# A GRU scan and a mixture of experts on one core: one scale for x, other chunk ends, and a step with its elementwise work dealt out anew

## The chip, the core and the metric

The kernel runs on one NeuronCore of a Trainium2 chip. The core has TensorE (PE, matrix products), VectorE (DVE), ScalarE (ACT, activation functions), GpSimd (POOL) and SyncE (SP), which here only issues DMA transfers. Each engine works through its own instructions in order; engines wait for each other by counting semaphores. The metric is the time of one launch in device microseconds.

## What is computed

The reference runs a GRU cell over x (4 x 512 x 512), started from `cond`, sends the states through a layer of four experts and adds the result to x:

```python
def cell(h, x):
    gi = x @ W_ih + b_ih
    gh = h @ W_hh + b_hh
    i_r, i_z, i_n = jnp.split(gi, 3, axis=-1)
    h_r, h_z, h_n = jnp.split(gh, 3, axis=-1)
    r = jax.nn.sigmoid(i_r + h_r)
    z = jax.nn.sigmoid(i_z + h_z)
    n = jnp.tanh(i_n + r * h_n)
    h_new = (1.0 - z) * n + z * h
    return (h_new, h_new)
...
for i in range(E):                       # E = 4 experts, the top 2 for each token, 512 tokens each
    sel_p, sel_idx = jax.lax.top_k(score, capacity)
    tok = flat_x[sel_idx]
    h = jax.nn.gelu(tok @ W1[i], approximate=False)
    y = h @ W2[i] * p
    out = out.at[sel_idx].add(y)
return x + out
```

## The kernel before

**Steps.** The 512 time steps of each of the 4 sequences are cut into 16 segments of 32 steps, and all 64 segments run at once as 64 columns. A segment starts from a guessed state, so 40 steps run before the 32 whose states are kept (`FIRST` = 40, `L` = 32, 72 in all), and a check at the end asks whether the segments' ends meet their neighbours' starts; only if not would further rounds of 32 steps run. The 512 hidden units are four blocks of 128 rows, j = 0 to 3. The states are held times a power of two, s.

**Numbers in halves.** Matrix products run in fp16. A number is kept as a high half and a low half (what the high one leaves). The first 20 steps (`ROUGH`) multiply high halves alone. From step 20 a step has 144 recurrent matmuls (128 x 64 columns, line 400): for each pair (j, k) six with the high half of state block k (`HIGH`, both halves of the weights, three gates) and three with its low half (`LOW`). The input gates r and z of the step, computed in advance, are added by a product with a diagonal matrix (`inject`, line 410: a matmul for the high and one for the low part, called a pair of injections here). `ORDER` writes out in what order TensorE takes these units.

**A step on the other engines.** When gate block j is complete, ScalarE makes the sigmoids r and z (`sig`, line 673), VectorE the product with r (`reset`, 1078) and the candidate's input (`candidate_in`, 1083), ScalarE the tanh (678), VectorE (z-1) times the candidate (`one_less_z`, 1087), GpSimd z times the old state (`carry`, 815). VectorE's `blend` (1094) gives the high half of the new state block, -s (z-1) n + z h, and releases the next step's `HIGH` units for this k; `keep_state` (1099) gives the same sum in fp32. The low halves are made by GpSimd for blocks 0 and 1 (823) and by VectorE for 2 and 3 (1118), as `LOW_BY = "PPDD"` says. Each engine has the order of these operations written out; TensorE waits for `high_ready`, `low_ready` and, before an injection, for `rn_done`.

**Input gates.** x @ W_ih for the step's inputs is computed in four chunks of 8 steps. The first chunk is done in fp32 at the start (lines 365 and 375); the rest, called the fill (line 392, 128 x 512), is spread over steps 0 to 22: 24 matmuls ahead of step 0, then 18 with each step, 13 of them at its head. ScalarE stores each finished tile (627, 630), VectorE makes its high half (`rz_high`, 986, a copy) and its low part (`rz_low`, 993); TensorE needs the high halves of a chunk when the chunk begins (steps 8, 16, 24), and from step 24 all low parts too. W_hh's low halves (`whh_low`, 1061) are made in twelve pieces between steps, as `WHH_AT` says. In all of these VectorE does the extra work after the step's own (`other_work`).

**Preparation.** Before anything is scaled, VectorE finds the largest magnitudes (944, 949, 959, 1010, 1029), GpSimd takes the maximum over partitions, and VectorE turns it into a power of two. x has two scales, `X0` for its first two chunks and `X1` for the others, so that the second is found later (1029).

**After the steps** come the transposition of the states, the choice of the tokens, and four experts with the products of lines 564 and 577. None of that is touched.

## Time and profile before

| | |
|---|---|
| three runs | 900.26, 902.24, 902.24 us (median 902.24) |
| the profiled execution | 901.38 us, span 899.6 us |
| PE busy | 808.9 us (90%) |
| DVE busy | 634.0 us (70%) |
| ACT busy | 414.9 us (46%) |
| POOL busy | 181.9 us (20%) |

The span is the time from the first to the last instruction, and the rest of an execution's time lies around it. The stages are: preparation up to 62.8 us, steps 0 to 19 and the filled steps 20 to 22 up to about 202, the plain steps up to about 459, then the choice of the tokens, and from 548 the experts. Matmuls are pipelined, so that a busy PE isn't one at its peak: the time between the starts of instructions tells more than their durations.

### The profile page before, as it was taken

How to read it: one execution, taken by the hardware profiler on the slowest of the kernel's cores; microseconds unless marked ns; L12 is line 12 of the kernel's file. 1: busy time of each engine (PE TensorE's matmuls, PEld its weight loads, DVE VectorE, ACT ScalarE, POOL GpSimd, SP SyncE). 2: the span in 40 equal slices, each digit the busy share in tenths (PEclk: the TensorE clock that was granted, in tenths of full speed). 3: DMA queues.
4: the chain of work that ended last, by engine and by line, in shares of the span. 5: the costliest groups of instructions: out<-in, count | busy, mean ns of one | idle time of the engine just before them, and what ended most of it. 6: DMA issues, size and time to landing. Idle time of an engine off the chain costs nothing.

```text
span 899.6 us, 28130 instructions
## 1 busy us (share of the span) xinstructions
PE 808.9 (90%) x11698; PEld 531.5 (59%) x11699; DVE 634.0 (70%) x2083; ACT 414.9 (46%) x852; POOL 181.9 (20%) x458
## 2 busy tenths in 40 slices
PE   7979899997999999999954147999999999999996
PEld 3436565687999899999944134444444444444442
DVE  5968898876888888888855865767666765774500
ACT  0767575653545545455423304834373257406600
POOL 1012121222433334333310010022002101120011
PEclk9999999998999999999978557999999999999999
DMA  8800000000000000000031740437152706350011
GB/s 322 333 0 3 2 2 1 2 3 3 4 5 4 4 4 4 5 4 4 4 131 60 226 174 24 141 95 211 24 182 63 210 12 202 84 169 13 1 24 23
DMA packets 20646, 62.58 MB, mean 70 GB/s; under 512 B 2160, under 2 KB 2160, under 8 KB 18032
## 3 DMA queue, kind: packets, MB, share of 16 engines
q1 hardware_dynamic: 16224, 52.47, 17.0%
q0 software_dynamic: 3584, 8.42, 5.2%
q8 instruction: 85, 1.39, 0.7%
q14 instruction: 33, 0.27, 0.1%
q10 hardware_dynamic: 720, 0.03, 0.1%
HBM read 52.49 MB, written 12.62 MB: 72 GB/s over the span
## 4 chain that ended last, share of the span: by engine, by line
PE 70%; DVE 20%; issue 5%; ACT 2%; DMA 1%; POOL 1%; DVEq 0%; SPq 0%; POOLq 0%
PE ps L564 19%; PE ps L577 18%; PE ps L400 18%; PE ps L392 8%; DVE wa L1078 4%; DVE wa L1083 3%; DVE halves L1094 3%; ACT wa L673 2%; PE ps L410 2%; PE ps L506 2%; DVE ocand L1087 1%; PE ps L552 1%; PE ps L544 1%; DMA big<-in_w_ih 1%; DVE chunk_peak L1010 1%
## 5 line engine op out<-in xcount | busy, mean ns | idle before, releaser
L400 PE MATMUL ps<-halves,wa 128*128 128x64 f16 x8448 | 289.8, 194 | 7.6 <-DVE halves L1094 1.4
L400 PEld LDWEIGHTS ps<-halves,wa 128*128 128x128 f16 x8448 | 273.4, 98 | 34.9 <-DVE halves L1094 15.9
L564 PE MATMUL ps<-wb,big 128*128 128x512 f16 x768 | 168.8, 382 | 1.5 <-DVE wb L1382 1.5
L577 PE MATMUL ps<-big 128*128 128x512 f16 x768 | 166.9, 379 | 0.0
L673 ACT ACTIVATE wa<-ps,un_gates 128x128 f32<-128x128 f32 x288 | 100.2, 366 | 126.5 <-PE ps L400 120.1
L564 PEld LDWEIGHTS ps<-wb,big 128*128 128x128 f16 x768 | 75.2, 98 | 93.1 <-issue 4.4
L577 PEld LDWEIGHTS ps<-big 128*128 128x128 f16 x768 | 75.2, 98 | 89.9
L678 ACT ACTIVATE wa<-wa,un_gates 128x64 f32<-128x64 f32 x288 | 99.1, 344 | 57.9 <-DVE wa L1083 51.4
L1078 DVE SCALAR_TENSOR_TENSOR wa<-ps,bhn_s,wa 128x64 f32<-128x64 f32 x288 | 80.0, 278 | 63.9 <-ACT wa L673 63.7
L392 PE MATMUL ps<-hx,wb 128*128 128x512 f16 x432 | 108.5, 384 | 4.9 <-issue 4.9
L740 ACT ACTIVATE hx<-ps,un_hid_in 128x512 f32<-128x512 f32 x64 | 43.7, 683 | 114.3 <-PE ps L564 112.0
L1094 DVE SCALAR_TENSOR_TENSOR halves<-ocand,neg_scale,wa 128x64 f16<-128x64 f32 (+1 forms) x288 | 86.5, 300 | 3.9
L1274 DVE SCALAR_TENSOR_TENSOR big<-wa,scale,big 128x2048 f16<-128x2048 f32 x28 | 65.3, 2350 | 26.0 <-ACT big L726 26.0
L726 ACT ACTIVATE big<-wa,scale 128x2048 f16<-128x2048 f32 x32 | 62.5, 1988 | 44.5 <-DVEq L1262 44.5
L1395 DVE SCALAR_TENSOR_TENSOR big<-hx,hid_scale,big 128x512 f16<-128x512 f32 x64 | 47.9, 749 | 44.3 <-ACT big L743 33.9
L1233 DVE TENSOR_REDUCE chunk_peak<-wa 128x1 f32<-128x2048 f32 x32 | 71.1, 2276 | 0.0
L410 PE MATMUL ps<-big,diag 128*128 128x128 f16 x496 | 62.4, 221 | 8.1 <-DVE big L986 8.0
L1083 DVE TENSOR_TENSOR wa<-wa,big 128x64 f32<-128x64 f32 x288 | 65.9, 229 | 5.1
L1087 DVE SCALAR_TENSOR_TENSOR ocand<-wa 128x64 f32<-128x64 f32 x288 | 62.6, 217 | 0.0
L392 PEld LDWEIGHTS ps<-hx,wb 128*128 128x128 f16 x432 | 38.4, 99 | 40.7 <-issue 7.9
L815 POOL TENSOR_TENSOR wa<-wa,hx 128x64 f32<-128x64 f32 x128 | 42.6, 333 | 78.6 <-ACT wa L673 74.0
L873 POOL DMA_INDIRECT out<-hx,idx_out x16 | 29.1, 1816 | 135.6 <-DVE hx L1401 135.6
(180 smaller groups left out, 685.7 us busy)
## 6 DMA issues: line engine op xcount, KB each, us to landing
wa<-in_w SPq DMA_DIRECT2D x32, 1024.0 KB, 7.3
hs_rows<-big SPq DMA_DIRECT2D x8, 516.0 KB, 6.4
hx<-in_x_t SPq DMA_DIRECT2D x3, 1024.0 KB, 18.6
big<-in_w_hh SPq DMA_DIRECT2D x4, 768.0 KB, 15.1
big<-in_w_ih SPq DMA_DIRECT2D x2, 1024.0 KB, 10.1
wa<-in_x_t SPq DMA_DIRECT2D x4, 256.0 KB, 4.8
big<-in_w_ih SPq DMA_DIRECT2D x4, 256.0 KB, 7.0
hx<-hs_rows,idx POOLq DMA_INDIRECT x16
```

Of the source, the lines that this page charges most:

```text
L392: mm = pe.matmul(ps[:, gi_bank(tile), :], wih_parts[:, w, k, m * P:(m + 1) * P], x_parts[:, q, t, k, :], start=(left == 0), stop=(left == ...
L400: mm = pe.matmul(gate_ps[:, j, g, :], whh_parts[:, k, w, (4 * g + j) * P:(4 * g + j + 1) * P], halves[:, src, k, h, :], start=False, stop= ...
L410: pe.matmul(gate_ps[:, j, 0:2, :], diag[:, 1 if c in (1, 2) else 0, :], gi_rz[:, c, j, part, :, cols], start=(part == HIGH), stop=False, s ...
L564: mm = pe.matmul(ps[:, m % 2, :], w1p[:, w, k, m * P:(m + 1) * P], tokT[:, t, k, :], start=(k == 0 and n == 0), stop=(k == KD - 1 and n == 2))
L577: mm = pe.matmul(ps[:, 2 + g % 2, :], hid[:, h, k, g * P:(g + 1) * P], w2p[:, w, k, :], start=(k == 0 and n == 0), stop=(k == KH - 1 and n ...
L673: act.activation(rz[:, j, :, :], gate_ps[:, j, 0:2, :], ACT.Sigmoid, scale=un_gates[:, 0:1]).then_inc(S["sig_done"], 1)
L678: act.activation(cand[:, j, :], cand_in[:, j, :], ACT.Tanh, scale=un_gates[:, 0:1]).then_inc(S["tanh_done"], 1)
L1078: dve.scalar_tensor_tensor(rn[:, j, :], gate_ps[:, j, 2, :], bhn_s[:, j:j + 1], rz[:, j, 0, :], ALU.add, ALU.mult).then_inc(S["rn_done"], 1)
L1083: dve.tensor_tensor(cand_in[:, j, :], rn[:, j, :], gi_n(j), ALU.add).then_inc(S["candin_ready"], 1)
L1087: dve.scalar_tensor_tensor(ocand[:, j, :], rz[:, j, 1, :], -1.0, cand[:, j, :], ALU.add, ALU.mult).then_inc(S["ocand_done"], 1)
L1094: dve.scalar_tensor_tensor(high_of(j), old(ocand_, j), neg_scale[:, 0:1], old(zh_, j), ALU.mult, ALU.add).then_inc(S["high_ready"], 1)
L1233: dve.tensor_reduce(chunk_peak[:, c:c + 1], stage[:, c * CHUNK:(c + 1) * CHUNK], AX.X, ALU.max, apply_absolute_value=True).then_inc(S["chu ...
```

## The change

Five things are done.

1. x has one scale (`XS`) for all chunks: all of x is loaded ahead of W_hh and its peak found ahead of the first scale; the late peak, the second gate scale and the second diagonal matrix go. The first x and W_ih loads go in halves instead of quarters, those of W_ih from ScalarE's queue.
2. ScalarE makes the high halves of five instead of eight tiles of the first chunk, VectorE the other three.
3. In the last step of a chunk the copy `rz_high` stands ahead of the step instead of behind it (`ahead`), and at the last filled step (23) `rz_low` too. W_hh's low pieces come one to a step, from step 0 on. The wait for all twelve pieces in ScalarE's step 16 becomes a wait in each of the tiles that overwrite them.
4. In the steps ScalarE makes s(1-z) = -s z + s (`kept_of`, tile `wz`, with scale and bias from columns), so that `one_less_z` is a plain product, and `blend` and `keep_state` plain sums. The product waits for `wz_done` as well.
5. GpSimd makes three of the four low halves, and `ORDER` and VectorE's order of a step are others.

```diff
-        ORDER = ((INJECT, 0, 0), (INJECT, 1, 0), (HIGH, 1, 0), (INJECT, 2, 0), (HIGH, 0, 0), (HIGH, 2, 0),
...
+        ORDER = ((INJECT, 2, 0), (INJECT, 0, 0), (INJECT, 1, 0), (HIGH, 1, 0), (HIGH, 0, 0), (HIGH, 2, 1), (INJECT, 3, 0),
...
-        WHH_AT = {5: (0, 1), 6: (2, 3), 7: (4, 5), 8: (6, 7), 13: (8, 9), 14: (10,), 15: (11,)}
+        WHH_AT = dict(zip((0, 1, 5, 6, 7, 8, 13, 14, 15, 16, 17, 18), range(WHH_PIECES)))
+        ACT_HIGHS = 5
-        LOW_BY = "PPDD"
+        LOW_BY = "PPPD"
...
+                def kept_of(j):
+                    act.wait_ge(S["sig_done"], base + j + 1)
+                    act.activation(wz[:, j, :], rz[:, j, 1, :], ACT.Identity, bias=scale[:, STATE:STATE + 1],
+                                   scale=neg_scale[:, 0:1]).then_inc(S["wz_done"], 1)
...
                 def one_less_z(j):
                     dve.wait_ge(S["tanh_done"], base + j + 1)
-                    dve.scalar_tensor_tensor(ocand[:, j, :], rz[:, j, 1, :], -1.0, cand[:, j, :],
-                                             ALU.add, ALU.mult).then_inc(S["ocand_done"], 1)
+                    dve.wait_ge(S["wz_done"], base + j + 1)
+                    dve.tensor_tensor(ocand[:, j, :], wz[:, j, :], cand[:, j, :], ALU.mult).then_inc(S["ocand_done"], 1)
                 def blend(j):
...
-                    dve.scalar_tensor_tensor(high_of(j), old(ocand_, j), neg_scale[:, 0:1], old(zh_, j),
-                                             ALU.mult, ALU.add).then_inc(S["high_ready"], 1)
+                    dve.tensor_tensor(high_of(j), old(ocand_, j), old(zh_, j), ALU.add).then_inc(S["high_ready"], 1)
...
-            for n in range(2, NC_):
-                dve.wait_ge(S["x_loaded"][n], 16)
-            link(dve.tensor_reduce(peak[:, X1:X1 + 1], hx[:, 2 * KD * GCOLS:KD * N], AX.X, ALU.max,
-                                   apply_absolute_value=True))
...
                 if i < FILLED:
                     for t in range(split_by(i - 1), split_by(i)):
                         if TILES[t][1] < 8:
-                            between += [(rz_high, t), (rz_low, t)]
+                            (ahead if s == STEPS_C - 1 else between).append((rz_high, t))
+                            (ahead if i == FILLED - 1 else between).append((rz_low, t))
```

ScalarE in a step, before: four sigmoids (L673 before, L670 after) and four tanhs (L678, L675).

```order
L673 ACTIVATE wa<-ps,un_gates 128x128 x3
L678 ACTIVATE wa<-wa,un_gates 128x64 x2
L673 ACTIVATE wa<-ps,un_gates 128x128
L678 ACTIVATE wa<-wa,un_gates 128x64 x2
```

And after:

```order
L670 ACTIVATE wa<-ps,un_gates 128x128 x2
L679 ACTIVATE wz<-wa,scale,neg_scale 128x64
L670 ACTIVATE wa<-ps,un_gates 128x128
L675 ACTIVATE wa<-wa,un_gates 128x64 x2
L679 ACTIVATE wz<-wa,scale,neg_scale 128x64
L670 ACTIVATE wa<-ps,un_gates 128x128
L675 ACTIVATE wa<-wa,un_gates 128x64
L679 ACTIVATE wz<-wa,scale,neg_scale 128x64 x2
L675 ACTIVATE wa<-wa,un_gates 128x64
```

The four new activations (L679) stand behind sigmoid 1, behind tanh 1, and two behind tanh 2.

TensorE in a plain step, before (L410 and L411 are injections, L400 and L401 recurrent matmuls):

```order
L410 MATMUL ps<-big,diag 128x128 x4
L400 MATMUL ps<-halves,wa 128x64 x6
L410 MATMUL ps<-big,diag 128x128 x2
L400 MATMUL ps<-halves,wa 128x64 x12
L410 MATMUL ps<-big,diag 128x128 x2
L400 MATMUL ps<-halves,wa 128x64 x126
```

And after:

```order
L411 MATMUL ps<-big,diag 128x128 x6
L401 MATMUL ps<-halves,wa 128x64 x18
L411 MATMUL ps<-big,diag 128x128 x2
L401 MATMUL ps<-halves,wa 128x64 x126
```

Three pairs of injections now stand ahead of the first unit. The last six of the 18 matmuls are `(HIGH, 2, 1)`, the first to need the second blend, so that it is wanted 12 matmuls behind the first one instead of 18. Behind its start 63 matmuls come until gate block 0 is complete, as before, but now with the last pair of injections among them. Behind gate block 0 there are 69 instead of 63; of these, blocks 1 and 2 are complete after 12 and 33 (before 15 and 27).

VectorE between steps 22 and 23, before: the low halves of step 22, copy and low part of one gate tile, and step 23's first reset; the last tile's copy and low part come behind step 23 in the same way.

```order
L1118 TENSOR_TENSOR halves<-carried,halves 128x64 x2
L986 CAST big<-gi_full 128x512
L993 TENSOR_TENSOR big<-gi_full,big 128x512
L1078 SCALAR_TENSOR_TENSOR wa<-ps,bhn_s,wa 128x64
L1083 TENSOR_TENSOR wa<-wa,big 128x64
```

And after, with both tiles ahead of step 23's first reset (L1068) and nothing behind its low half:

```order
L1106 TENSOR_TENSOR halves<-carried,halves 128x64
L987 CAST big<-gi_full 128x512
L994 TENSOR_TENSOR big<-gi_full,big 128x512
L987 CAST big<-gi_full 128x512
L994 TENSOR_TENSOR big<-gi_full,big 128x512
L1068 SCALAR_TENSOR_TENSOR wa<-ps,bhn_s,wa 128x64
L1073 TENSOR_TENSOR wa<-wa,big 128x64
```

## Rows read from the trace of the kernel before

**Rows 1.** windows by stage: length, busy us of each engine, granted clock, DMA share, GB/s

```profile
48.30:62.80 14.50, 9.64 (x38) 4.06 (x38) 9.06 (x21) 10.15 (x13) 2.78 (x5) 0.88 0.00 1
62.80:181.10 118.30, 114.67 (x1503) 71.00 (x1502) 100.17 (x387) 73.01 (x198) 24.69 (x82) 1.00 0.01 2
```

**Rows 2.** chain of waits, steps 20 and 49: start us, us, what

```profile
179.21 3.67 PE ps L400 x126
182.89 3.88 PE ps L392 x18
...
339.20 0.11 PE ps L410 x2
```

**Rows 3.** timeline, ScalarE in one plain step: start us, us

```profile
336.68 1.15 ACT L673 ACTIVATE wa<-ps,un_gates 128x128 f32<-128x128 f32 x3 [1.60 <-PE ps L400]
337.74 0.73 ACT L678 ACTIVATE wa<-wa,un_gates 128x64 f32<-128x64 f32 x2
...
341.78 1.16 ACT L673 ACTIVATE wa<-ps,un_gates 128x128 f32<-128x128 f32 x3 [1.60 <-PE ps L400]
```

**Rows 4.** timeline, VectorE and GpSimd in that step

```profile
337.13 1.13 POOL L815 TENSOR_TENSOR wa<-wa,hx 128x64 f32<-128x64 f32 x3 [1.60 <-ACT wa L673]
...
338.19 0.21 DVE L1087 SCALAR_TENSOR_TENSOR ocand<-wa 128x64 f32<-128x64 f32 x1
...
338.51 0.28 DVE L1094 SCALAR_TENSOR_TENSOR halves<-ocand,neg_scale,wa 128x64 f16<-128x64 f32 x1
...
339.24 0.41 DVE L1094 SCALAR_TENSOR_TENSOR halves<-ocand,neg_scale,wa 128x64 f16<-128x64 f32 x1
339.27 0.30 POOL L823 TENSOR_TENSOR halves<-hx,halves 128x64 f16<-128x64 f32 x1
```

**Rows 5.** groups by shape: xcount, busy us, mean ns, idle before

```profile
L678 ACT ACTIVATE wa<-wa,un_gates 128x64 f32<-128x64 f32 x192 | 65.8, 343 | 36.5 <-DVE wa L1083 34.4
...
L627 ACT ACTIVATE gi_full<-ps,bias_gi,gi_scale 128x512 f32<-128x512 f32 x8 | 6.1, 767 | 25.0 <-DVEq L980 22.0 <-DVE big L993 2.9
...
L627 ACT ACTIVATE gi_full<-ps,bias_gi 128x512 f32<-128x512 f32 x2 | 1.4, 688 | 2.1 <-PE ps L392 1.9 <-issue 0.3
```

**Rows 6.** timeline, step 0 and the chunk ends at steps 8 and 16

```profile
65.49 0.88 ACT L673 ACTIVATE wa<-ps,un_gates 128x128 f32<-128x128 f32 x3 [4.56 <-PE ps L400]
...
69.17 0.29 DVE L1094 SCALAR_TENSOR_TENSOR halves<-ocand,neg_scale,wa 128x64 f16<-128x64 f32 x1
...
109.39 0.23 PE L410 MATMUL ps<-big,diag 128*128 128x128 f16 x1 [2.31 <-DVE big L986]
...
150.60 0.89 ACT L673 ACTIVATE wa<-ps,un_gates 128x128 f32<-128x128 f32 x3 [0.70 <-PE ps L400]
...
157.61 0.88 ACT L673 ACTIVATE wa<-ps,un_gates 128x128 f32<-128x128 f32 x3 [3.13 <-PE ps L400]
```

**Rows 7.** timeline and a window, the chunk end at step 24

```profile
201.95 1.16 ACT L673 ACTIVATE wa<-ps,un_gates 128x128 f32<-128x128 f32 x3 [0.36 <-PE ps L400]
...
206.91 0.42 DVE L986 CAST big<-gi_full 128x512 f16<-128x512 f32 x1
...
208.16 0.58 PE L410 MATMUL ps<-big,diag 128*128 128x128 f16 x4 [4.42 <-DVE big L986]
...
208.00:214.00 6.00, 5.84 (x103) 5.87 (x103) 0.06 (x1) 0.37 (x1) 0.03 (x1) 0.50 0.01 3
...
218.92 0.37 ACT L673 ACTIVATE wa<-ps,un_gates 128x128 f32<-128x128 f32 x1 [1.60 <-PE ps L400]
```

**Rows 8.** chain of waits, then timeline, preparation

```profile
12.21 2.29 DVE chunk_peak L944
...
38.77 4.41 DVE L1029 TENSOR_REDUCE peak<-hx 128x1 f32<-128x4096 f32 x1
...
51.67 1.41 DVE L1004 SCALAR_TENSOR_TENSOR hx<-hx,scale 128x512 f16<-128x512 f32 x2
...
53.18 9.83 PE L392 MATMUL ps<-hx,wb 128*128 128x512 f16 x37 [4.86 <-issue]
```

More of the change, by code:

```diff
@@ L31 @@
 HIDDEN_TO = float(2.0 ** -16)
-WHH, STATE, W1, W2, WIH, X0, BIAS, X1 = range(8)
+WHH, STATE, W1, W2, WIH, XS, BIAS = range(7)
 SEARCH_BITS = 3
@@ L211, in gru_moe @@
         S["wih_loaded"] = [sem(f"wih_loaded_{g}") for g in range(3)]
-        S["first_loaded"] = [sem(f"first_loaded_{k}") for k in range(KD)]
+        S["first_loaded"] = [sem(f"first_loaded_{k}") for k in range(2)]
         S["whh_loaded"] = [sem(f"whh_loaded_{k}") for k in range(KD)]
-        S["x_loaded"] = [sem(f"x_loaded_{n}") for n in range(NC_)]
+        S["x_loaded"] = [sem(f"x_loaded_{n}") for n in range(1, NC_ + 1)]
         block = ctx.enter_context(nc.Block())
@@ L302, in _ @@
         def _(sp):
-            for k in range(KD):
-                sp.dma_start(x_first[:, k, :], x_t[:, CHUNK_ORDER[0], k, :]).then_inc(S["first_loaded"][k], 16)
-                sp.dma_start(wih_sb[:, k, 0:D], wih_src[:, k, 0:D]).then_inc(S["first_loaded"][k], 16)
+            for k in range(2):
+                sp.dma_start(x_first[:, 2 * k:2 * k + 2, :], x_t[:, CHUNK_ORDER[0], 2 * k:2 * k + 2, :]
+                             ).then_inc(S["first_loaded"][k], 16)
             for g in range(1, 3):
@@ L409, in inject @@
                 for part in parts:
-                    pe.matmul(gate_ps[:, j, 0:2, :], diag[:, 1 if c in (1, 2) else 0, :], gi_rz[:, c, j, part, :, cols],
+                    pe.matmul(gate_ps[:, j, 0:2, :], diag[:, :], gi_rz[:, c, j, part, :, cols],
                               start=(part == HIGH), stop=False, skip_group_check=True)
@@ L591, in _ @@
         def _(act):
+            for k in range(2):
+                act.dma_start(wih_sb[:, 2 * k:2 * k + 2, 0:D], wih_src[:, 2 * k:2 * k + 2, 0:D]
+                              ).then_inc(S["first_loaded"][k], 16)
             act.dma_start(bih[:, :], b_ih).then_inc(S["small_loaded"], 16)
@@ L617, in x_high, with keep_tile @@
                 act.activation(x_parts[:, q, HIGH, k, :], xT[:, q + 1, k, :], ACT.Copy,
-                               scale=x_scale(q)).then_inc(S["x_high"], 1)
-            def keep_tile(t, q, sc, g_sc):
+                               scale=scale[:, XS:XS + 1]).then_inc(S["x_high"], 1)
+            def keep_tile(t, sc, g_sc):
                 c, m = TILES[t]
@@ L651, in _ @@
                 first_tile(m)
+                first_high(m)
             for k in range(KD):
                 wih_high(k)
-            act.wait_ge(S["x_loaded"][1], 16)
             for k in range(KD):
                 x_high(0, k)
-            first_tile(3)
-            first_tile(4)
+            for m in range(3, ACT_HIGHS):
+                first_tile(m)
+                first_high(m)
             act.wait_ge(S["gates_known"], 1)
-            whh_high(0)
-            first_tile(5)
-            whh_high(1)
-            first_tile(6)
-            whh_high(2)
-            first_tile(7)
-            whh_high(3)
-            for m in range(8, 12):
+            for k in range(KD):
+                whh_high(k)
+            for m in range(ACT_HIGHS, 12):
                 first_tile(m)
@@ L1062, in whh_low, with step @@
                                          whh_parts[:, k, HIGH, cols], ALU.mult, ALU.subtract).then_inc(S["whh_ready"], 1)
-            def step(gi_n, after, src, base, low, moved=False, between=()):
+            def step(gi_n, after, src, base, low, moved=False, ahead=(), between=()):
                 dst = 1 - src
@@ L1127, in step @@
                          (one_less_z, 2), (blend, 2), (one_less_z, 3), (blend, 3), (other_work, 0))
+                for f, n in ahead:
+                    f(n)
                 for n, (f, j) in enumerate(exact if low else rough):
@@ L1165, in _ @@
                     after = lambda j, i=i: hs[:, j, i - FIRST + 1, :]
-                between = []
+                ahead, between = [], []
                 if i < FILLED:
@@ L1169, in _ @@
                         if TILES[t][1] < 8:
-                            between += [(rz_high, t), (rz_low, t)]
+                            (ahead if s == STEPS_C - 1 else between).append((rz_high, t))
+                            (ahead if i == FILLED - 1 else between).append((rz_low, t))
                 if 1 <= s <= KD and q < 2:
                     between.append((x_low, (q + 1, s - 1)))
-                for n in WHH_AT.get(i, ()):
-                    between.append((whh_low, n))
-                step(lambda j, c=c, cols=cols: gi[:, c, j, 2, cols], after, i % 2, KD * i, i >= ROUGH - 1, moved, between)
+                if i in WHH_AT:
+                    between.append((whh_low, WHH_AT[i]))
+                step(lambda j, c=c, cols=cols: gi[:, c, j, 2, cols], after, i % 2, KD * i, i >= ROUGH - 1, moved, ahead, between)
             def run(steps):
```

152 lines of the change are left out of this document (72 added, 80 removed).

## The prediction

> **What bounds the kernel now.** The table of windows comes first: through the filling steps (62.80 to 181.10) TensorE counts as busy for 114.7 of 118.3 us at full granted clock, while at the end of the preparation (48.30 to 62.80) it is busy for only 9.6 of 14.5 us, at 0.88 [rows 1]. A busy TensorE is not the answer by itself, so the second view is one plain step (24 to 71). A recurrent matmul costs 0.029 us (126 in 3.67), a filling matmul 0.216 (18 in 3.88), a pair of injections 0.11 [rows 2]. A plain step has 144 recurrent matmuls and 4 pairs: 144 x 0.0291 + 0.45 = 4.65 us. The sigmoids of row block 0 start 5.10 us apart [rows 3]. So 0.45 us of each plain step are waits: the step is bound by a loop (gate 0 finished, sigmoid, reset, candidate, tanh, blend, matmuls again), with TensorE's own work close behind.
>
> The loop is read from the time of the step's first sigmoid. The second blend starts at 339.24 - 336.68 = 2.56 and takes 0.41 instead of the 0.28 of the first, while GpSimd's low half runs from 339.27 [rows 4]. It ends at 2.97, TensorE sees it 0.06 later, at 3.03, and 63 matmuls (1.84) and 0.2 us of matmul and semaphore latency bring the next sigmoid: 5.10 with 0.03 of small waits.
>
> The steps that also fill the input gates cost 18 x 0.216 + 48 x 0.029 + 4 x 0.055 = 5.51 us on TensorE and last 5.51: there TensorE is the bound, and nothing that VectorE saves there shows. The exceptions are the chunk ends. At the first TensorE idles 2.31 us for a VectorE copy; from the sixteenth sigmoid to the seventeenth it is 7.01 us, 1.50 above the period [rows 6]. At the third TensorE idles 4.42 us, until VectorE's last copy and low part of the gates are done, and then runs at 0.50 of its clock from 208 to 214: the two steps from 201.95 to 218.92 take 16.97 us instead of 10.20, 6.8 too many [rows 7]. The preparation has a gap of 4.86 us before the filling matmuls, which then run partly at half clock [rows 8, 1].
>
> **The change, part by part.**
>
> *Preparation.* One scale for all of x replaces two. VectorE's late reduction over two chunks (4.41 us) and its waits go (4.6 in all), about 0.2 us of single-column work is left in its place, and one low part (0.6) moves behind the x parts. VectorE's last x part ended at 51.67 + 1.41 = 53.08 [rows 8]; 53.1 - 4.6 - 0.6 + 0.2 = 48.1. But the reductions of x move ahead of the first scale: 4096 more columns at 4.41 / 4096 us, 4.4 us more VectorE work there. Most of it fits into the time up to 12.21 in which VectorE waits for all of the first eight loads; I put everything behind it 1.0 us later (bounds 0 and 2.5), so the last x part is ready at 49.1. TensorE's fp32 products end at 53.18 - 4.86 = 48.32 now; with the first loads twice as large they start later, I take 1.5 us (bounds 0.5 and 3): 49.8. This becomes the bound. Then 24 + 13 filling matmuls at full clock take 8.0 and the last one's tail 0.2, to 58.0, against 53.18 + 9.83 = 63.0 now: **-5.0** (-3 to -6.5). ScalarE's queue holds the same tiles less three copies (these go to VectorE, behind the x parts) and hides behind these matmuls. The full clock rests on the gap being under 1 us: the gap of 2.31 us at 109 left the clock at 1.00, those of 4.42 and 4.86 were followed by half clock [rows 1, 6 to 8].
>
> *Loads.* The w_hh pieces now land behind all of x. VectorE reduces them after the x peaks anyway; this is part of the 1.0. The copy x to out starts after the same bytes: nothing.
>
> *Chunk ends.* The copy for the first and second chunk goes ahead of the last step, and w_hh's low parts are spread one to a step. In a filling step VectorE's last blend ends 69.17 + 0.29 - 65.49 = 3.97 behind the sigmoid, 3.5 behind its own first reset, so 2 us are left in 5.51 [rows 6]; a copy with its low part (from 206.91 to the restart less 0.1: 1.15 [rows 7]) and one w_hh part (0.7 by the same low part, an estimate) fit. TensorE finds both copy and blend within its 13 filling matmuls: -2.4 and -1.5, together **-3.9**. At the third, the pair goes ahead of step 23, which has no fill to hide it: 1.05 us of delay (the pair, less what of it VectorE had free) against 6.8: **-5.7**. That TensorE then idles about 1.5 us costs no clock, by the 2.31 us gap. If the half clock stayed (6 us at 0.50, so 3 lost), it would be -2.7.
>
> *Plain steps.* ScalarE gains four activations with two operands per partition. The 64-column one with one such operand takes 343 ns, and the second operand is worth 767 - 688 = 79 ns at 512 columns [rows 5]: 0.42 us, of which the next one starts after 0.33. Bounds: 0.34 (no surcharge) and 0.77 (the 512-column row). Four make 1.3 us more on ScalarE, which idles 1.60 us before a step's first sigmoid [rows 3]. Their place matters more. In the new order gate 2 is finished 33 matmuls after gate 0, not 27, and its sigmoid starts at 0.96, ahead of tanh 0 (before at 1.06). Sigmoid-to-tanh distance is 0.27 (third sigmoid 336.68 + 1.15 - 0.37 = 337.46, tanh 337.74), so tanh 0 starts at 1.22, tanh 1 at 1.48, the activation for block 1 at 1.73, ending at 2.15. The product that replaces the 1-z form now waits for two semaphores; such a pair costs 0.10 behind the work awaited (blend: 338.51 - 338.19 - 0.21) [rows 4]. Behind it in VectorE's queue wait the blend and the next reset. So: product 2.25, second blend 2.57, the old 2.56. ScalarE's help and the old form meet the loop at the same moment.
>
> From there: the plain sum takes 0.22, as the two-input form without an operand per partition does (0.21 at 338.19 [rows 4]), not 0.28. Does it still collide with GpSimd? Sigmoid 3 follows the block-1 activation, at 2.06, and GpSimd's product starts 0.45 behind it (337.13 - 336.68 [rows 4, 3]), at 2.51, 0.06 before the blend. I take 0.11 for the collision (trace: 0.13; bounds 0 and 0.27). The blend ends at 2.90, against 2.97: -0.07. But behind the unit that waits for it TensorE now has 63 matmuls and one pair of injections: +0.11. And the high half of block 3 is wanted 6 matmuls earlier than before while VectorE delivers it later (reset 3 stands behind the blend, tanh 3 behind two of the new activations): +0.06. **5.20 us a step, +0.10; 48 steps: +4.8** (bounds: rivals B and D). Saved VectorE time itself (0.06 on each of eight sums, 0.22 for the low half that GpSimd takes) is off this loop and counts for nothing. If sigmoid 2 no longer got in the way, the gain would be up to 0.26.
>
> A rule speaks against more two-input sums beside more GpSimd work: the Trainium skill, SBUF — State Buffer, "SBUF: two separate sides", says that a VectorE instruction with two SBUF inputs and a GpSimd one that reads SBUF lock each other out for the whole instruction. The trace agrees that they collide but shows 0.13 us, not GpSimd's 0.30; by the rule the step would be 5.36, which is rival C's price.
>
> *The rest.* The search, the experts and the end are untouched. The first expert starts partly at half clock, which can shift by 1 to 2 us either way.
>
> **Sum.** -5.0 - 3.9 - 5.7 + 4.8 = -9.8 on the profiled execution of 901.38 (span 899.6): 891.6. That execution lies within the runs shown (900.26 to 902.24, median 0.9 above it), so I give 891.5. A measurement here tells about 0.3% (2.7 us) from no change.
>
> **The rivals.**
> - B, the steps get shorter (0.17): no collision and no wait for block 3. For it: a distance of 0.06 us decides, and the first blend of the same step (0.28) is clear of GpSimd [rows 4]. Against: both engines get more to do in that span. 5.20 - 0.11 - 0.07 = 5.02, -0.08 x 48: -14.6 - 3.8 = -18.4, 883.
> - C, the collision costs the whole GpSimd instruction (0.12): the blend waits until 2.84, the end of GpSimd's product (0.33): 5.36. +0.26 x 48 = 12.5: -2.1, 899.3. For it: a third low half adds GpSimd work. Against: the 0.13 of the trace.
> - D, ScalarE turns it slower (0.06): the activation for block 1 stands alone between tanh 1 and its product, so each 0.1 us on it is 0.1 us a step. It turns the sign when a step costs 14.6 / 48 = 0.30 more than before, that is with 0.63 us instead of 0.42. At 0.77 the step is 5.55: +21.6, in all +7.0, 908.
> - E, the preparation gains little (0.14): the paired loads land late, as the eight first loads did (VectorE waited until 12.21 [rows 8]), and the reductions, 2.2 us for 2048 columns, queue up behind. -2 instead of -5: 894.6. For it: 4.4 us more work in front. Against: VectorE now starts with the first pair.
> - F (0.01): s(1-z) rounded otherwise trips the check of the states, and a round of 32 steps, 166 us, is added.
>
> **Numbers.** Forecast 0.50, own range 888 to 895.5. Range for 8 in 10: 883.5 to 899; what is left out is half of B, D, F and the edge of C. Faster by over 0.3%: A, B, E and half of C, 0.87; within: 0.06; slower, D, F and a rest: 0.07.
>
> **What would show it.** Step 0's first injection at about 58 and no low clock ahead of it; sigmoid distances of 5.51 at the first two chunk ends and about 6.2 at the third, clock 1.00; distances of 5.20 in the plain steps, the second blend at 2.6 behind the sigmoid with TensorE's longest wait for it; the new activation at 0.42. Wrong if the plain step falls under 5.05 or rises over 5.35, or if the gap before the filling matmuls stays over 3 us.

## The result, and the profile after

The changed kernel takes 893.33 us (median of 4 runs, 892.45 to 894.43); the kernel before, run beside it, 901.73 us (900.26 to 902.24). The ratio is 0.991, with a 95% interval of 0.9892 to 0.9928. The forecast was 891.5, its own range 888 to 895.5. The span of the profiled execution is 890.6 us, 9.0 less than before.

The distances between the starts of block 0's sigmoids, one per step, say where the time went:

| stretch | before | after | difference | forecast |
|---|---|---|---|---|
| start of step 0's sigmoid | 65.49 | 61.35 | -4.14 | -5.0 |
| step 1 to step 2 | 5.51 | 6.23 | +0.72 | 0 |
| step 7 to 8 | 7.99 | 5.99 | -2.00 | -2.4 |
| step 15 to 16 | 7.01 | 5.51 | -1.50 | -1.5 |
| step 19 to 20 | 6.96 | 7.37 | +0.41 | 0 |
| step 23 to 25 | 16.97 | 11.91 | -5.06 | -5.7 |
| step 25 to 71 (46 steps) | 235.23 | 237.53 | +2.30 | +4.8 (48 steps) |

That makes -9.27 of the -9.24 found at step 71; the rest of the run is 0.2 us longer. The rows are these. First the timeline of ScalarE in the kernel after (start us, us, engine, line, ... idle before and what ended it), the sigmoids of steps 1, 2, 7, 8, 23 and 25, to be read against [rows 6, 7]:

```profile
66.86 0.62 ACT L670 ACTIVATE wa<-ps,un_gates 128x128 f32<-128x128 f32 x2 [0.45 <-PE ps L401]
73.09 0.62 ACT L670 ACTIVATE wa<-ps,un_gates 128x128 f32<-128x128 f32 x2 [0.27 <-PE ps L401]
...
100.63 0.62 ACT L670 ACTIVATE wa<-ps,un_gates 128x128 f32<-128x128 f32 x2 [0.30 <-PE ps L401]
106.62 0.62 ACT L670 ACTIVATE wa<-ps,un_gates 128x128 f32<-128x128 f32 x2 [0.89 <-PE ps L401]
...
195.47 0.37 ACT L670 ACTIVATE wa<-ps,un_gates 128x128 f32<-128x128 f32 x1 [0.17 <-PE ps L401]
...
207.38 0.72 ACT L670 ACTIVATE wa<-ps,un_gates 128x128 f32<-128x128 f32 x2 [1.41 <-PE ps L401]
```

The windows of the kernel after (length, busy us of each engine, granted clock, DMA share, GB/s) answer to [rows 1]: the end of the preparation has TensorE busy for 13.32 of 14.60 us and at full clock, where it was at 0.88.

```profile
44.00:58.60 14.60, 13.32 (x50) 5.74 (x49) 11.16 (x15) 12.14 (x14) 2.70 (x5) 1.00 0.00 1
58.60:177.00 118.40, 117.46 (x1562) 73.06 (x1560) 101.09 (x396) 96.07 (x286) 27.23 (x86) 1.00 0.01 2
```

The chain of waits at the same place, and from VectorE's timeline its last two x parts: the fp32 products end at 49.45, the last x part at 49.22 + 1.41 = 50.63, and the fill starts 1.28 us behind the products and runs for 8.15. Of [rows 8] the gap was 4.86 us and the fill 9.83.

```profile
43.87 5.58 PE ps L376 x13
49.45 1.28 issue
50.73 8.15 PE ps L393 x37
...
49.22 1.41 DVE L1005 SCALAR_TENSOR_TENSOR hx<-hx,scale 128x512 f16<-128x512 f32 x2
```

And the chain in a plain step (48, its first sigmoid at 326.27):

```profile
328.20 0.23 DVE halves L1084
...
328.51 0.23 DVE ocand L1078
...
328.84 0.31 DVE halves L1084
...
329.19 0.35 PE ps L401 x6
329.54 0.13 PE ps L411 x2
329.67 1.69 PE ps L401 x57
...
331.39 0.72 ACT wa L670 x2
```

The product of block 1 starts 2.24 us behind the sigmoid (forecast 2.25), the second blend at 2.57 (2.57), TensorE goes on at 2.92, and 63 matmuls with one pair of injections fill the 2.2 us to the next sigmoid at 5.12 (5.20). The groups of the page give the new activation 430 ns (forecast 0.42 us), and the plain sum 237 ns over all its 288 executions, 0.225 us where nothing collides:

```profile
L679 ACT ACTIVATE wz<-wa,scale,neg_scale 128x64 f32<-128x64 f32 x288 | 116.7, 430 | 0.0
...
L1084 DVE TENSOR_TENSOR halves<-ocand,wa 128x64 f16<-128x64 f32 (+1 forms) x288 | 68.3, 237 | 10.7 <-DVE ocand L1078 0.9
```

### The profile page after: what moved, and what is told of

It is laid out like the page before. It is cut to its first block, busy times and chain, and to the rows that moved or that the text cites. A ratio compares the mean times of both kernels' runs of the same rounds, so it can differ in the third digit from the quotient of the medians.

```text
span 890.6 us, 28701 instructions
## 1 busy us (share of the span) xinstructions
PE 805.3 (90%) x11698; PEld 532.3 (60%) x11699; DVE 619.5 (70%) x2028; ACT 486.6 (55%) x1137; POOL 199.8 (22%) x510
## 3 DMA queue, kind: packets, MB, share of 16 engines
q1 hardware_dynamic: 15504, 51.42, 16.7%
## 4 chain that ended last, share of the span: by engine, by line
PE 62%; DVE 17%; ACT 13%; issue 5%; DMA 1%; DVEq 1%; POOL 0%; POOLq 0%; ACTq 0%
PE ps L565 19%; PE ps L578 19%; PE ps L401 12%; ACT wa L670 6%; ACT wa L675 4%; ACT wz L679 3%; DVE halves L1084 3%; PE ps L376 3%; DVE ocand L1078 3%; PE ps L393 2%; DVE wa L1073 2%; PE ps L507 2%; PE ps L366 2%; DVE big L994 2%; DVE wa L1068 1%
## 5 line engine op out<-in xcount | busy, mean ns | idle before, releaser
L401 PE MATMUL ps<-halves,wa 128*128 128x64 f16 x8448 | 289.3, 194 | 10.2 <-DVE halves L1084 10.1
L401 PEld LDWEIGHTS ps<-halves,wa 128*128 128x128 f16 x8448 | 271.0, 98 | 34.1 <-DVE halves L1084 16.0
L670 ACT ACTIVATE wa<-ps,un_gates 128x128 f32<-128x128 f32 x288 | 101.2, 362 | 93.4 <-PE ps L401 93.4
L679 ACT ACTIVATE wz<-wa,scale,neg_scale 128x64 f32<-128x64 f32 x288 | 116.7, 430 | 0.0
L1068 DVE SCALAR_TENSOR_TENSOR wa<-ps,bhn_s,wa 128x64 f32<-128x64 f32 x288 | 80.4, 279 | 49.2 <-ACT wa L670 49.0
L675 ACT ACTIVATE wa<-wa,un_gates 128x64 f32<-128x64 f32 x288 | 93.3, 341 | 12.2 <-DVE wa L1073 7.8
L1084 DVE TENSOR_TENSOR halves<-ocand,wa 128x64 f16<-128x64 f32 (+1 forms) x288 | 68.3, 237 | 10.7 <-DVE ocand L1078 0.9
L1078 DVE TENSOR_TENSOR ocand<-wz,wa 128x64 f32<-128x64 f32 x288 | 64.1, 223 | 10.6 <-ACT wz L679 4.6
```

Source lines behind the costliest of these rows:

```text
L401: mm = pe.matmul(gate_ps[:, j, g, :], whh_parts[:, k, w, (4 * g + j) * P:(4 * g + j + 1) * P], halves[:, src, k, h, :], start=False, stop= ...
L670: act.activation(rz[:, j, :, :], gate_ps[:, j, 0:2, :], ACT.Sigmoid, scale=un_gates[:, 0:1]).then_inc(S["sig_done"], 1)
L675: act.activation(cand[:, j, :], cand_in[:, j, :], ACT.Tanh, scale=un_gates[:, 0:1]).then_inc(S["tanh_done"], 1)
L679: act.activation(wz[:, j, :], rz[:, j, 1, :], ACT.Identity, bias=scale[:, STATE:STATE + 1], scale=neg_scale[:, 0:1]).then_inc(S["wz_done"], 1)
L1068: dve.scalar_tensor_tensor(rn[:, j, :], gate_ps[:, j, 2, :], bhn_s[:, j:j + 1], rz[:, j, 0, :], ALU.add, ALU.mult).then_inc(S["rn_done"], 1)
L1078: dve.tensor_tensor(ocand[:, j, :], wz[:, j, :], cand[:, j, :], ALU.mult).then_inc(S["ocand_done"], 1)
```

## The experiments

**The step undone.** The changed kernel with the step of before.

```diff
-                for f, j in ((sig, 0), (sig, 1), (kept_of, 0), (sig, 2), ...
+                for f, j in ((sig, 0), (sig, 1), (sig, 2), (tanh, 0), (tanh, 1), (sig, 3), (tanh, 2), (tanh, 3)):
...
-                    dve.tensor_tensor(ocand[:, j, :], wz[:, j, :], cand[:, j, :], ALU.mult) ...
+                    dve.scalar_tensor_tensor(ocand[:, j, :], rz[:, j, 1, :], -1.0, cand[:, j, :], ...
# and the same for blend, keep_state, LOW_BY = "PPDD", ORDER, VectorE's order
```

> The changed kernel with the step of before put back whole (forms of product and sums, orders of TensorE, VectorE and ScalarE, two low halves each on GpSimd and VectorE); preparation, loads, chunk ends and the places of w_hh's low parts stay changed. Theory: the new step costs 0.03 us in an ordinary plain step (5.12 against 5.09) and has six stretched ones, 2.3 us over the 46 plain steps from the 25th on, and the last blend of a filled step comes 0.4 us earlier again, so that of the 0.72 us lost behind step 1 and the 0.48 at step 8 about 0.9 goes: 893.3 - 2.3 - 0.9 = 890.1 us. Rival 1, the prediction's own term (4.8 us for the steps): 888.5. Rival 2, the new step helps or is neutral and the traces differ by chance: 893.3 or more.

Measured: 889.35 us (887.36 to 890.13), ratio 0.9867 (0.985 to 0.9883). Steps 25 to 71 take 235.75 us against 237.53, step 1 to 2 takes 5.58 against 6.23, step 7 to 8 5.51 against 5.99. So the new step costs most of 4 us: 1.8 in the plain steps, 1.1 in the filled ones, where its longer ScalarE queue delays VectorE's last products, and 0.3 at steps 20, 24 and 25. Another 0.5 is the start of step 0, at 60.87 here and at 61.35 in the changed kernel; seven profiled kernels with the same preparation have it between 60.62 and 61.35, so that this lies within their spread. Preparation and chunk ends alone are worth 12 us: with the step left as it was the kernel would have been faster than the changed one.

**The step alone**, on the kernel before.

The edit is the kernel before with `ORDER`, `kept_of`, the plain product and sums, `LOW_BY = "PPPD"` and the orders of ScalarE and VectorE of the changed kernel, as in the diff of the change. Preparation, loads, chunk ends and `WHH_AT` are untouched.

> The kernel before with the changed step alone (plain product and sums, ScalarE's s(1-z), three low halves on GpSimd, the new orders); preparation, loads, chunk ends as before. Theory: 46 plain steps at 5.12 with some stretched ones, +2.3, nothing in the filled steps or up to 1: 904.0 to 905.0 us. Rival 1, the prediction's 0.10 us a step: 906.5. Rival 2, the step is no slower: 901.7 or less.

Measured: 907.44 us (906.94 to 907.99), ratio 1.0063 (1.0046 to 1.0079): 6.1 more than before, over the 904 to 905 expected and over the rival's 906.5. The plain steps are as expected (5.12, some longer). The loss that was not expected is mostly at the first two chunk ends: 9.99 us from sigmoid 7 to 8 (before 7.99) and 9.24 from 15 to 16 (before 7.01); 23 to 25 got shorter, 15.87 (before 16.97). TensorE's timeline and the granted clock behind the two gaps:

```profile
110.29 0.23 PE L410 MATMUL ps<-big,diag 128*128 128x128 f16 x1 [2.82 <-DVE big L992]
...
158.53 0.23 PE L410 MATMUL ps<-big,diag 128*128 128x128 f16 x1 [1.94 <-DVE big L992]
```
```profile
112.00:114.00 2.00, 2.00 (x21) 1.20 (x19) 0.28 (x1) 0.00 (x0) 0.00 (x0) 0.50 0.00 0
160.00:162.00 2.00, 2.00 (x23) 1.34 (x22) 0.00 (x0) 0.00 (x0) 0.00 (x0) 0.50 0.00 0
```

Both fell to 0.50, the lower of the two levels (1.2 GHz), while the gap of 2.31 us of [rows 6] had left the clock at 1.00. So the two halves of the change are not additive: the step is dearer (6.1 against 4.0 us) with the old chunk ends.

**VectorE's extra work dealt out anew.**

```diff
-        WHH_AT = dict(zip((0, 1, 5, 6, 7, 8, 13, 14, 15, 16, 17, 18), range(WHH_PIECES)))
+        WHH_STEPS = (1, 5, 7, 8, 13, 14, 15, 16, 17, 18, 19, 19)
...
-            pe.wait_ge(S["whh_ready"], WHH_PIECES)
             for i in range(ROUGH, FIRST + L):
                 if i < FILLED:
                     fill(filled(i), filled(i + 1))
+                if i == ROUGH:
+                    pe.wait_ge(S["whh_ready"], WHH_PIECES)
...
-            x_low((0, 0))
-            x_low((0, 1))
+            for k in range(KD):
+                x_low((0, k))
             rz_low(3)
-            x_low((0, 2))
-            x_low((0, 3))
```

> The changed kernel with three places rearranged: w_hh's low parts go to steps 1, 5, 7, 8, 13 to 18 and two to 19 (none to 0 and 6), TensorE waits for the last of them behind the fill of step 20 and not ahead of it, and VectorE's low part of tile 3 goes behind all four x parts in the preparation. Theory: VectorE's extra work of steps 0 (2.8 us) and 6 was more than the 2 us that a filled step leaves it. -0.7 behind step 1, -0.5 at step 8, -0.4 at step 20, -0.7 ahead of the fill: 893.3 - 2.3 = 891.0 us. Rival: the losses at steps 1 and 8 come from ScalarE's longer queue (the last product waits for it), not from the amount of extra work; then only steps 20 and the fill gain, 1.1, and the time is 892.2.

Measured: 896.23 us (895.78 to 896.70), ratio 0.994 (0.9923 to 0.9956), slower than the changed kernel by 2.9. Two of the four gains are there to the hundredth: step 1 to 2 takes 5.51, step 7 to 8 takes 5.51. Step 0 starts at 60.58, which is no more than the edge of what the kernels without this edit show (60.62 to 61.35). The fourth turned over: step 19 to 20 takes 11.85 instead of 7.37. Two pieces behind step 19's own work end after TensorE has run out of fill; it waits 3.6 us, and the next 4 us run at 0.65:

```profile
173.04 0.51 PE L411 MATMUL ps<-big,diag 128*128 128x128 f16 x6 [3.62 <-DVE wa L1050]
```
```profile
173.00:177.00 4.00, 3.96 (x85) 3.96 (x86) 0.00 (x0) 0.00 (x0) 0.00 (x0) 0.65 0.01 4
```

**The third chunk end undone.**

```diff
-                            (ahead if s == STEPS_C - 1 else between).append((rz_high, t))
-                            (ahead if i == FILLED - 1 else between).append((rz_low, t))
+                            (ahead if s == STEPS_C - 1 and i < FILLED - 1 else between).append((rz_high, t))
+                            between.append((rz_low, t))
```

> The changed kernel with the last pair of copy and low part of the third chunk back behind step 23's own work (the first two chunk ends stay ahead). Theory: TensorE waits 4.2 us again, its clock falls to half for some 6 us behind it, and the two steps from the sigmoid of step 23 on last about 17 us instead of 11.9: +5.0, 898.3 us, with a granted clock of about 0.5 in the stretch behind the wait. Rival: with the new step's shorter VectorE queue the wait stays under the length that turned the clock, and only the wait itself comes back: +2 to +2.5, 895.5 us, clock 1.00.

Measured: 897.88 us (896.17 to 899.21), ratio 0.9959 (0.9942 to 0.9976). The two steps take 16.73 us instead of 11.91. The theory holds, half clock included (898.3 expected):

```profile
202.05 0.80 PE L411 MATMUL ps<-big,diag 128*128 128x128 f16 x6 [4.65 <-DVE big L994]
```
```profile
202.00:206.00 4.00, 3.95 (x67) 3.98 (x68) 0.00 (x0) 0.00 (x0) 0.00 (x0) 0.50 0.00 0
```

**ScalarE's new activation twice, for block 1.**

```diff
+                def spare(j):
+                    act.wait_ge(S["sig_done"], base + j + 1)
+                    act.activation(wz_spare[:, :], rz[:, j, 1, :], ACT.Identity, ...)
-                for f, j in (... (tanh, 1), (kept_of, 1), (sig, 3),
+                for f, j in (... (tanh, 1), (spare, 1), (kept_of, 1), (sig, 3),
```

> The changed kernel in which ScalarE makes s(1-z) of block 1 twice in every step, once into a spare buffer that nobody reads, right ahead of the real one. It measures the price of ScalarE time at the place the prediction put on the loop. Theory: the first of the pair holds ScalarE for 0.33 us, the product of block 1 (now 2.24 us behind the sigmoid) and the second blend move by as much less the 0.02 to 0.1 us of slack that the trace shows, so 0.25 to 0.32 us a step, 48 steps: +12 to +15.5, and up to 1 us more in the VectorE-bound filled steps: 906 to 909.5 us. Rival: VectorE's own queue (first blend, then the product) sets the time and ScalarE has room: under 0.1 us a step, 898 at most.

Measured: 916.04 us (914.97 to 916.41), ratio 1.016 (1.0142 to 1.0178), over the 906 to 909.5 expected. The plain step is 5.45: 0.33 more, the whole of the activation, so 15.8 us over 48. The filled steps, where I had allowed 1 us in all, rose from 5.51 to about 5.72 each and hold most of the rest: with 0.33 us more on ScalarE they too are bound by the loop, through ScalarE and VectorE's extra work, and no more by TensorE. The chain of a plain step now runs through it:

```profile
342.14 0.33 ACT wz_spare L685
342.48 0.34 ACT wz L680
...
342.91 0.23 DVE ocand L1084
```

**TensorE's order of before in the changed kernel.**

```diff
-        ORDER = ((INJECT, 2, 0), (INJECT, 0, 0), (INJECT, 1, 0), (HIGH, 1, 0), ...
+        ORDER = ((INJECT, 0, 0), (INJECT, 1, 0), (HIGH, 1, 0), (INJECT, 2, 0), ...
```

> The changed kernel with TensorE's written order of before, everything else changed. The prediction charged the new order with 0.11 us a step for a pair of injections and possibly 0.06 for an earlier block 3. Theory A (these are real and stand alone): the step gets shorter by 0.11, 5.01 us, -5.3 us: 888 us. Theory B (the order was made for ScalarE's longer queue; with the old one gate 2's sigmoid comes at another place between ScalarE's operations and tanh 1 and the activation of block 1 later): up to 0.15 us a step more, 5.27, +7: 900 us. I hold B likelier.

Measured: 903.86 us (902.32 to 905.02), ratio 1.0029 (1.0019 to 1.0039). It went theory B's way, but by more than its 0.15: plain steps of 5.34, 0.22 more. Its chain shows why. The sigmoids of blocks 1 and 2 come 0.08 to 0.09 later and push everything behind them on ScalarE, but the second blend only by 0.06. The larger part was in neither theory: VectorE's order stayed that of the changed kernel, where reset 3 stands behind the second blend, and in TensorE's old order an injection waits for it ahead of the units that need that blend, 0.21 us more:

```profile
334.08 0.30 DVE halves L1085
334.38 0.21 DVE wa L1069
334.59 0.05 issue
334.63 0.29 PE ps L412 x2
```

So the 0.22 us are the price of two orders that don't fit each other, and not of TensorE's order by itself.

**GpSimd's fourth product later**, out of the second blend's way.

```diff
                 for j in range(KD):
+                    if low and j == KD - 1:
+                        pool.wait_ge(S["state_done"], base + (1 - KD * (ROUGH - 1)))
                     carry(j)
```

> The changed kernel in which GpSimd's product z h of block 3 waits until VectorE has kept state block 0, so that it starts at about 2.66 us behind the sigmoid and not 0.10 us ahead of the second blend. Theory: the second blend takes 0.225 us like the others, not 0.300; 0.075 us a step less, 5.04 to 5.05 us, 48 steps: -3.6, 889.7 us. Rival 1: the low half of block 0, now 0.25 us later, is late for TensorE and the gain is lost: 893. Rival 2: the blend is long for another reason (it waits for two semaphores, or what it writes) and stays at 0.300: 893.

Measured: 899.43 us (898.54 to 900.47), ratio 0.9974 (0.9964 to 0.9984). The blend does fall to 0.23 us, and the step still grows to 5.25. VectorE's timeline, and GpSimd's, whose two low halves (L821) start at 332.08 and 332.38 (x2 is two instructions):

```profile
331.70 0.23 DVE L1086 TENSOR_TENSOR halves<-ocand,wa 128x64 f16<-128x64 f32 x1
...
332.16 0.33 DVE L1075 TENSOR_TENSOR wa<-wa,big 128x64 f32<-128x64 f32 x1
332.42 0.34 DVE L1080 TENSOR_TENSOR ocand<-wz,wa 128x64 f32<-128x64 f32 x1
```
```profile
332.08 0.59 POOL L821 TENSOR_TENSOR halves<-hx,halves 128x64 f16<-128x64 f32 x2
```

Each of two collisions now costs VectorE 0.12 to 0.13 where one had cost 0.075; blends 2 and 3 come 0.16 and 0.12 us later and TensorE waits for both. I had named a late low half as the rival; it was the next two VectorE operations.

**The old step with GpSimd's first low half later.** The first experiment's kernel with three edits.

```diff
                 if low:
+                    pool.wait_ge(S["rn_done"], base + 2 * KD)
                     for j in range(POOL_LOWS):
# the w_hh wait behind the fill of step 20 and rz_low(3) behind the x parts, as above
```

> The kernel with the old step and the changed preparation and chunk ends, with three more edits: GpSimd's first low half waits for VectorE's reset 3 (it then starts at about 2.72 us behind the sigmoid and not at the same moment as the second blend), TensorE's wait for w_hh's last low part stands behind the fill of step 20, and VectorE's low part of tile 3 behind the four x parts. Theory: the second blend falls from 0.41 to 0.28 us, plain steps from 5.09 to 4.97: -6; the fill starts 0.7 earlier and step 20 gains 0.2 to 0.4: 889.4 - 6.9 = 882.5 us. Rival: the low half comes too late for TensorE's tenth unit, or the next VectorE operation collides in the blend's place: steps stay at 5.05 to 5.10, 887 to 888.5 us.

Measured: 888.80 us (888.02 to 889.39), ratio 0.986 (0.9842 to 0.9877): no better than the 889.35 without these edits, within their spread, where 882.5 was expected. Again the blend did what was asked, 0.28 us instead of 0.41, and the step stayed at 5.09. VectorE's timeline, and behind the dots the same sum (L1067) in the first experiment's kernel, without these edits:

```profile
326.30 0.28 DVE L1080 SCALAR_TENSOR_TENSOR halves<-ocand,neg_scale,wa 128x64 f16<-128x64 f32 x1
326.49 0.36 DVE L1069 TENSOR_TENSOR wa<-wa,big 128x64 f32<-128x64 f32 x1
...
328.08 0.41 DVE L1104 TENSOR_TENSOR halves<-hx,halves 128x64 f16<-128x64 f32 x2
...
326.55 0.21 DVE L1067 TENSOR_TENSOR wa<-wa,big 128x64 f32<-128x64 f32 x1
```

The rival that was written down beforehand came: the sum behind the blend now meets GpSimd's low half in its place (0.36 us for 0.21), so what the blend gave is taken back in VectorE's queue, whose last low half ends 4.75 us behind the sigmoid with and without the edits.

TensorE starts its row 0.13 us earlier and loses it again at one spot: matmuls mostly start 0.03 us apart; the distance of 0.155 us ahead of the first one with high half 1 is gone, and one of 0.125 stands ahead of the first with low half 3, which VectorE finishes last (328.08 + 0.41 = 328.49). Windows of 0.12 us around that spot show it by the number of matmuls in flight, 10, then 6:

```profile
328.27:328.40 0.13, 0.13 (x10) 0.13 (x7) 0.13 (x2) 0.00 (x0) 0.00 (x0) 1.00 0.00 0
328.42:328.54 0.12, 0.12 (x6) 0.07 (x3) 0.07 (x1) 0.00 (x0) 0.00 (x0) 1.00 0.00 0
```

So before the change the step had two bounds of nearly one length: the second blend, and the end of VectorE's queue.

**Plain sums for blocks 2 and 3 alone**, on top of that kernel.

```diff
+                    if j >= 2:
+                        dve.wait_ge(S["wz_done"], base + 2 * (j - 1))
+                        dve.tensor_tensor(ocand[:, j, :], wz[:, j, :], cand[:, j, :], ALU.mult) ...
+                        return
                     dve.scalar_tensor_tensor(ocand[:, j, :], rz[:, j, 1, :], -1.0, cand[:, j, :], ...
# blend and keep_state likewise; ScalarE: ... (sig, 3), (tanh, 2), (kept_of, 2), (kept_of, 3), (tanh, 3)
```

> The last kernel (joined), in which VectorE's last low half had turned out to be what TensorE waits for once the second blend is 0.13 us earlier, with one more edit: blocks 2 and 3 alone get the plain product and sums (s(1-z) by ScalarE, behind tanh 2 and ahead of tanh 3, where ScalarE is idle for 0.8 us), blocks 0 and 1 keep the form of before. Theory (two bounds of nearly one length: the second blend's matmuls and VectorE's end): four sums are 0.06 us shorter, so the last low half is ready about 0.18 us earlier, the wait of 0.125 ahead of its matmuls goes, and the plain step falls from 5.09 to 4.97: 48 x 0.125 = 6.0, 882.8 us. Rival 1: the double waits of these products eat the gain on VectorE, steps stay at 5.09, 888.8. Rival 2: VectorE's end was not the bound and the step is limited by something that neither edit touches: 888.8 with the gap ahead of the same matmuls.

Measured: 883.73 us (881.93 to 884.18), ratio 0.9802 (0.978 to 0.9825), faster than both kernels, 9.6 us under the changed one and 5.1 under the one that it was built on (6.0 expected). The plain step is 4.97, as forecast; some more steps are stretched. VectorE's last two low halves end at 324.85 + 0.41 - 320.67 = 4.59 behind the sigmoid (joined: 4.76), and TensorE's wait is gone (11 matmuls in such a window):

```profile
324.85 0.41 DVE L1121 TENSOR_TENSOR halves<-hx,halves 128x64 f16<-128x64 f32 x2
```
```profile
325.00:325.12 0.12, 0.12 (x11) 0.12 (x8) 0.12 (x2) 0.00 (x0) 0.00 (x0) 1.00 0.00 0
```

The plain sums without the later low half were not run, so that VectorE's end shortened by itself is not shown to bring nothing.

**Four more waits on VectorE**, to move the holes that stretch a step now and then.

```diff
+                if low:
+                    for k in range(4):
+                        dve.wait_ge(S["gi_kept"], 12 + k)
                 for n, (f, j) in enumerate(exact if low else rough):
```

> The changed kernel with four more VectorE instructions in every step from the 19th on: waits that were satisfied long before, ahead of reset 0, where VectorE idles 0.8 us. The question is what stretches one plain step in eight by 0.14 to 0.35 us, with a hole in VectorE's queue where nothing is awaited. Theory (VectorE's instructions are loaded in pieces of fixed size, and a hole comes where a piece ends): the holes, now at multiples of about 22 us, come closer together, by 34 instructions a step for 30, at about 19.5 us, and in other steps; the ordinary step stays at 5.12; 893 to 895 us. Rival: the holes come from something that recurs in time or on another engine (DMA, semaphores): they stay where they were, in the same steps.

Measured: 910.00 us (909.04 to 910.53), ratio 1.0098 (1.0072 to 1.0125), 16.7 more than the changed kernel, with a plain step of 5.51 and no stretched one. The expectation (5.12, 893 to 895) missed the direct cost. The waits themselves sit in idle time, but reset 0 now starts 0.50 us behind the sigmoid instead of 0.40, its own wait having become an instruction of its own, and both candidates behind it meet a product of GpSimd (0.38 and 0.39 instead of 0.23):

```profile
334.50 0.28 DVE L1068 SCALAR_TENSOR_TENSOR wa<-ps,bhn_s,wa 128x64 f32<-128x64 f32 x1 [0.85 <-ACT wa L670]
334.82 0.38 DVE L1073 TENSOR_TENSOR wa<-wa,big 128x64 f32<-128x64 f32 x1
...
335.42 0.39 DVE L1073 TENSOR_TENSOR wa<-wa,big 128x64 f32<-128x64 f32 x1
```
```profile
334.44 0.67 POOL L813 TENSOR_TENSOR wa<-wa,hx 128x64 f32<-128x64 f32 x2 [0.97 <-ACT wa L670]
335.41 0.32 POOL L813 TENSOR_TENSOR wa<-wa,hx 128x64 f32<-128x64 f32 x1 [0.29 <-ACT wa L670]
```

0.10 + 0.15 + 0.16 = 0.41, against 0.39 measured. What it says on the holes stands in the last section.

## Why the prediction was right, and where not

**The total.** Preparation, chunk ends and plain steps all went the forecast way, but the total is nearer than its parts, and that is luck. Ahead of the plain steps 11.6 us were gained and not 14.6, and the plain steps cost 2.3 us and not 4.8. These two misses, 3.0 and 2.5 us, have opposite signs and nearly cancel.

**Preparation, -5.0: -4.14.** The mechanism and the clock held: one gap of 1.28 us in place of 4.86, and full clock. TensorE's fp32 products end at 49.45 (forecast 49.8). The missed part is the last x part: it ends at 50.63 and not 49.1, so VectorE and not TensorE is the bound. The low part of tile 3, 0.69 us between the x parts, may be a part of it, but that isn't settled: in the three kernels with it moved behind them step 0 starts at 60.58, 60.77 and 60.90, 0.3 us earlier on the mean than in the seven others, and within their spread of 0.7.

**Chunk ends 8 and 16, -3.9: -3.5.** Step 16 was exact. At step 8 0.48 stayed, and with it belongs the 0.72 behind step 1, which the forecast did not have. The failed step is that 2 us are left in a filled step of 5.51 and that a copy with its low part and one w_hh part fit. Step 0 has two pairs, not one: 2 x 1.06 + 0.71 = 2.8 us, as its chain shows:

```profile
65.72 0.35 DVE big L987
...
66.09 0.69 DVE big L994
66.79 0.35 DVE big L987
...
67.16 0.69 DVE big L994
67.85 0.71 DVE wa L1051
```

And the new step itself leaves less room there than the old one, from whose [rows 6] the 2 us were taken: with the old step and the same extra work, 0.65 of the 0.72 and all of the 0.48 go. With the new step and less extra work (nothing of w_hh in steps 0 and 6) both go too. The 0.41 at step 20 is the wait for the last w_hh part, placed one step before its use; "one to a step" costs nothing only where it ends in time. With the wait behind the fill and the old step, that distance is back at 6.96.

**Chunk end 24, -5.7: -5.06.** Undoing it brings 4.8 us of two steps back, wait and half clock both. Sigmoid 24 comes 1.6 us later than in a plain step and not 1.05: step 22's pair stands behind that step's own work, right ahead of the one that was moved, and takes VectorE's free time. Full clock followed the gap of 1.17 us, as the forecast had it. But its reason, that a gap under 2.31 us costs no clock, is wrong as a rule: in the second experiment one of 1.94 did.

**Plain steps, +4.8: +2.3.** The sign and the loop were right, and each place on it within 0.02 us up to the second blend. Two terms were too large, and one was missing. The collision cost 0.075, not 0.11. The +0.06 for a high half of block 3 that is wanted 6 matmuls earlier did not happen: behind the second blend TensorE waits for nothing. With these two put right the forecast would have been 5.10 to 5.11; 5.12 was measured, 0.03 above before. Missing were the stretched steps: seven of the 46 are 0.09 to 0.35 us longer, 1.6 us in all (before there was 0.4 of this kind). That ScalarE's activation stands on the loop with no slack (0.33 us for 0.33) was as said; the injection pair (+0.11) is right as a count (63 matmuls and a pair in the 2.20 us of the chain), but putting TensorE's order back alone does not return it.

**The rivals.** B (no collision, 5.02) and C (0.26 a step more) are both out: there is a collision, and it costs what the distance leaves. C was what follows from the Trainium skill, SBUF — State Buffer, "SBUF: two separate sides", a lock for the whole instruction. No run here shows that: the collisions measured are 0.075 to 0.16 us beside GpSimd instructions of 0.30 to 0.36. D's price was right, 0.33 us a step for 0.33, but its condition did not come (430 ns). E did not come: the gain in the preparation was 4.14. F did not come either; no round was added.

That the time saved on VectorE "is off this loop and counts for nothing" fits the change as made, where TensorE waits for nothing behind the second blend. It would not have held for the next edit: in the old step, once the second blend is 0.13 us earlier, VectorE's end is the bound, and 0.17 us saved there are worth 0.125 a step.

What stays open: how TensorE's clock chooses between gaps of 2.31 us (kept) and 1.94 us (fell). It wasn't tried apart from the steps around them.

## What to carry to other kernels

Where two waits of nearly one length close the same loop, shortening the one that the trace names can show nothing, as here (888.80 for 889.35 us). Look for the wait that appears in its place before calling an edit worthless, then take both. And work moved into another engine's idle time is priced by where it stands in that engine's queue: 0.33 us of ScalarE between tanh 1 and its product costs 0.33 a step; behind tanh 2, where ScalarE was idle, two of the same kind leave tanh 3 where it was (3.14 us behind the sigmoid) and were part of a gain of 5.1 us.

## What the runs showed of the hardware

*VectorE beside GpSimd.* A VectorE sum, product or difference of two SBUF tiles that starts shortly behind the start of a GpSimd product or difference ends as if it had started 0.17 to 0.20 us behind GpSimd's start. Delay and lag add up to nearly the same: lag 0.02 and 0.02 us, +0.15 and +0.16 (four more waits); 0.04, +0.13, and 0.08, +0.12 (fourth product later); 0.10, +0.075 (after); at a lag of 0.19 nothing was added (after, the product at 327.87 beside GpSimd's at 327.68: 0.225 us). Being ahead is no safe place for every form: the blend of the kernel before, with a column operand, starts 0.03 us ahead of GpSimd's low half and is 0.13 longer all the same [rows 4]. VectorE's resets, one input of which lies in PSUM, were not stretched at such places.

*Holes in VectorE's queue.* In the kernel after VectorE stops now and then for some 0.3 us with nothing to wait for. With ScalarE's spare activation, the same VectorE program runs up to 22 us later by the clock and stops in the same steps at the same instructions; here the first of them, after and with the spare activation:

```profile
222.04 0.23 DVE L1084 TENSOR_TENSOR halves<-ocand,wa 128x64 f16<-128x64 f32 x1 [0.32 <-issue]
```
```profile
229.47 0.22 DVE L1090 TENSOR_TENSOR halves<-ocand,wa 128x64 f16<-128x64 f32 x1 [0.32 <-issue]
```

In the kernel after they lie on a grid of about 22 us, or 4.3 steps of 30 VectorE instructions (waits of their own included), which is 128 instructions. Counted in the trace in steps of 128 from the instruction at 222.04, the places fall into steps 27, 32, 36, 40, 44, 49, 53, 57, 61, 66 and 70, and the seven stretched steps (27, 36, 44, 53, 57, 61, 70) are all among them; at the other four no step is longer. Within 0.8 us of each of the eleven the profile has a transfer of instructions of 8 KB (222.7, 266.5, 355.1, 376.1, 398.5 among them), of 19 such transfers between 205 and 450. In the first experiment the grid is 24.2 us, 4.76 steps of 27: 128 again. With four more waits it is 22.0 us, 4.00 steps of 32 (as the trace lists them, not the 34 of the expectation): 128, and not the 19.5 us expected. The place then falls at the same spot of every fourth step, and neither a hole nor a stretched step is seen there; why it costs nothing at that spot is not shown. That run alone doesn't tell a count from a time, since its 22.0 us are also those of the kernel after; the spare activation (23.5 us) and the first experiment (24.2) do. So they go by the count of instructions and not by time. That it is the loading of VectorE's code fits, but no run showed the loading itself to be the cause.
